# Graph and attention kernel: one block-limit number per group, group release signalled by VectorE, edge weights summed panel by panel

## What is computed

```python
def _rgcn_conv(x, src, dst, etype, W, root, b):
    x_src = x[src]
    seg = dst * num_rel + etype
    sums = jax.ops.segment_sum(x_src, seg, num_segments=num_nodes * num_rel)
    cnt = jax.ops.segment_sum(jnp.ones((src.shape[0],), dtype=x.dtype), seg, num_segments=num_nodes * num_rel)
    mean = sums / jnp.maximum(cnt, 1.0)[:, None]
    mean = mean.reshape(num_nodes, num_rel, -1)
    out = jnp.einsum('nri,rio->no', mean, W)
    return out + x @ root + b
```

## Time and profile before

| | |
|---|---|
| median of 3 runs | 3418.33 us (3415.06 to 3421.1) |
| the profiled execution's own time | 3421.39 us |
| its span, first to last instruction | 3419.5 us |
| edge stage of layer 0 | 650.97 to 1064.3 us of the span |
| edge stage of layer 1 | 1629.93 to 2047.0 us |
| granted TensorE clock, mean | 0.979 |

### The profile page before, as it was taken

How to read it: one execution, slowest core, us unless ns; L and a number is a source line. 1 busy time by engine, 2 the same in 40 slices (tenths; PEclk the granted TensorE clock), 3 DMA queues, 4 the chain that set the end, 5 groups by cost and what they waited for, 6 DMA issues and landing times.

```text
span 3419.5 us, 64810 instructions
## 1 busy us (share of the span) xinstructions
PE 3174.5 (93%) x19556; PEld 2359.9 (69%) x19557; DVE 1773.6 (52%) x2941; ACT 762.8 (22%) x1086; POOL 1273.2 (37%) x1377
## 2 busy tenths in 40 slices
PE   6999999999997999999899989999886999999999
PEld 5788888777776888888677766776654555555555
DVE  7576666555555333333555552334586456455551
ACT  2211121000001212211000004444212543543540
POOL 2681000577772000002777761000420632652562
PEclk9999999999999999999999999999998999999999
DMA  5334334599994232321898882000330000000003
GB/s 149 101 106 149 118 116 137 171 306 307 306 306 140 87 120 94 118 95 63 319 307 307 303 287 78 14 28 14 88 95 24 20 1 19 19 1 19 19 28 95
DMA packets 101141, 433.58 MB, mean 127 GB/s; under 512 B 19648, under 2 KB 19971, under 8 KB 96818
## 3 DMA queue, kind: packets, MB, share of 16 engines
q0 software_dynamic: 55712, 266.87, 23.2%
q1 hardware_dynamic: 42593, 124.83, 11.6%
q10 hardware_dynamic: 2736, 40.50, 3.4%
HBM read 355.21 MB, written 76.88 MB: 126 GB/s over the span
## 4 chain that ended last, share of the span: by engine, by line
PE 71%; DVE 12%; issue 7%; DVEq 6%; ACT 1%; POOL 1%; DMA 1%; POOLq 0%; SPq 0%; ACTq 0%
PE PS L1466 26%; PE PS L1580 13%; PE PS L1776 5%; PE PS L1604 3%; PE PS L1711 3%; PE PS L1475 3%; DVE NM L1387 2%; PE PS L1612 2%; PE PS L1759 2%; PE PS L1760 2%; PE PS L1715 2%; PE PS L1649 2%; DVE HOT L1166 2%; PE PS L1633 2%; PE PS L1623 1%
## 5 line engine op out<-in xcount | busy, mean ns | idle before, releaser
L1466 PE MATMUL PS<-WHL,XT 128*125 (+1 forms) x3240 | 549.4, 329 | 7.0 <-DVE WHL L940 4.2
L1466 PE MATMUL PS<-WHL,HT 128*125 (+1 forms) x3240 | 531.8, 327 | 0.0
L1580 PE MATMUL PS<-GATA,HOT 128*125 128x384 f16 x2880 | 492.6, 328 | 37.0 <-issue 17.8
L1466 PEld LDWEIGHTS PS<-WHL,XT 128*125 (+1 forms) x3240 | 441.3, 138 | 92.7 <-issue 5.3
L1466 PEld LDWEIGHTS PS<-WHL,HT 128*125 (+1 forms) x3240 | 441.9, 137 | 84.2
L558 POOL DMA_INDIRECT GATA<-msg_table,SKEY x432 | 421.8, 976 | 163.0 <-issue 124.6
L1580 PEld LDWEIGHTS PS<-GATA,HOT 128*125 x2880 | 386.3, 137 | 114.5 <-issue 44.6
L1166 DVE SCALAR_TENSOR_TENSOR HOT<-NODE,DSTF,WHLO x720 | 297.0, 475 | 277.6 <-issue 277.6
L594 POOL TENSOR_TENSOR PL<-PF 125x500 bf16<-125x500 f32 (+1 forms) x360 | 320.6, 924 | 281.0 <-ACT PF L797 277.8
L1016 DVE SCALAR_TENSOR_TENSOR MSG<-PS,MSG 125x768 f16<-125x768 f32 x160 | 153.1, 957 | 360.3 <-ACT MSG L627 358.9
L627 ACT ACTIVATE MSG<-PS 125x768 f16<-125x768 f32 x160 | 129.6, 810 | 786.8 <-PE PS L1466 773.9
(11 more groups left out here) (254 smaller groups left out, 3898.6 us busy)
## 6 DMA issues: line engine op xcount, KB each, us to landing
msg_table<-MSG SPq DMA_DIRECT2D x160, 336.0 KB
WST<-in_wg_dram ACTq DMA_DIRECT2D x16, 2304.0 KB, 10.1
WST<-in_wf_dram SPq DMA_DIRECT2D x7, 1536.0 KB, 6.3
KROW<-key_rows POOLq DMA_DIRECT2D x54, 192.0 KB, 3.8
GATA<-msg_table,SKEY POOLq DMA_INDIRECT x432, 4.5
msg_table<-MSG SPq DMA_DIRECT2D x160, 39.0 KB
WST<-in_wm_dram SPq DMA_DIRECT2D x5, 1152.0 KB, 5.1
GATB<-msg_table,SKEY POOLq DMA_INDIRECT x216, 4.5
```

What stands on the lines that cost most here:

```text
L1466: ins = pe.matmul(PS[0:ROWS, b0 + h, 0:HALF], X[:, xp, k, bass.ts(t, ROWS)], panel_part(slot, wp, k, h), start=k == 0 and xp + wp == 0, st ...
L1580: ins = pe.matmul(PS[0:ROWS, bass.ds(((n + (L + 1)) % 2) * 2 + h, 1), 0:HALF].rearrange("p a c -> p (a c)"), HOT[:, bass.ds((n % 2) * AT + ...
```

## The change

- `LIM` holds one number for a group, first block times 10 plus last block; `group_blocks` makes one load and then splits the number in registers with a division and a remainder. This is done by TensorE and by VectorE. `block_limits` computes the packed number once.
- The one-column matmul at the end of a group is gone. VectorE raises `group_used` when it leaves the loop over the group's blocks, and once more after the last take; a group counts as released for GpSimd when the count shows that VectorE has left the loop of the group after it (`grp - GSETS + 2`).
- The drain of VectorE's loop stands now in `take_pass`, behind the `HOT` tiles instead of ahead of them.
- The edge weights are summed by one relation at a time (`relation_weight`): in layer 0 inside the loop that loads the key rows, four relations in panel 3 and then one in each panel, in layer 1 as each panel's scale is ready. When all are there, one multiplication brings them to the common scale (`common_weight`), and three instructions (`edge_weights`) finish. In layer 0 these three come after the first group's four gathers.
- In this diff the order of the nine panels is as before.

```diff
@@ group_blocks
-            return (eng.value_load(LIM[0:1, bass.ds(g, 1)], min_val=0, max_val=RT - 1),
-                    eng.value_load(LIM[0:1, bass.ds(g + AG, 1)], min_val=1, max_val=RT))
+            both = eng.value_load(LIM[0:1, bass.ds(g, 1)], min_val=0, max_val=RT * RT - 1)
+            return both // RT, both % RT + 1
@@ gpsimd
+            def relation_weight(L, r):
+
+                g.wait_ge(S["relation_in"], L * REL + r + 1)
+                g.sem_inc(S["pool_tick"], 1)
+                if r == 0:
+                    g.tensor_scalar(WSUM[:], ETF[:, 0:TILES], 0.0, GW[:, 0:1], ALU.is_equal, ALU.mult)
+                else:
+                    g.tensor_scalar(TMPF[:], ETF[:, 0:TILES], float(r), GW[:, r:r + 1], ALU.is_equal, ALU.mult)
+                    g.drain()
+                    g.tensor_tensor(WSUM[:], WSUM[:], TMPF[:], ALU.add)
+                g.drain()
+
+            def common_weight(L):
 
                 g.wait_ge(S["relations_made"], L + 1)
                 g.sem_inc(S["pool_tick"], 1)
-                g.tensor_scalar(WSUM[:], ETF[:, 0:TILES], 0.0, GW[:, REL:REL + 1], ALU.is_equal, ALU.mult)
-                for r in range(1, REL):
-                    g.tensor_scalar(TMPF[:], ETF[:, 0:TILES], float(r), GW[:, REL + r:REL + r + 1], ALU.is_equal, ALU.mult)
-                    g.drain()
-                    g.tensor_tensor(WSUM[:], WSUM[:], TMPF[:], ALU.add)
-                    g.drain()
+                g.tensor_scalar(WSUM[:], WSUM[:], GS[:, 1:2], None, ALU.mult)
+                g.drain()
+
+            def edge_weights(L):
+
...
+                if u % RT == RT - 1:
+                    p = COUNTED + u // RT
+                    for r in range(0 if p == COUNTED else p, p + 1):
+                        relation_weight(0, r)
+
             for L in range(2):
-                edge_weights(L)
+                if L == 1:
+                    for r in range(REL):
+                        relation_weight(1, r)
+                common_weight(L)
+                if L == 1:
+                    edge_weights(1)
...
+                    if L == 0 and t == AT:
+                        edge_weights(0)
                     if t % AT == 0:
                         if grp >= GSETS:
-                            g.wait_ge(S["group_used"], AG * L + grp - GSETS + 1)
+                            g.wait_ge(S["group_used"], (AG + 1) * L + grp - GSETS + 2)
...
@@ vector
-                v.tensor_scalar(LIM[:, 0:AG], PS[0:1, 5, 0:AG], -1.0, None, ALU.add)
-                v.tensor_copy(LIM[:, AG:2 * AG], PS[0:1, 5, AG:2 * AG])
+                v.tensor_scalar(GBT[:], PS[0:1, 5, 0:2 * AG], -1.0, None, ALU.add)
+                v.drain()
+                v.scalar_tensor_tensor(LIM[:], GBT[:, 0:AG], float(RT), GBT[:, AG:2 * AG], ALU.mult, ALU.add)
...
-                    v.tensor_copy(GW[:, bass.ds(p, 1)], SC[:, WINV])
+                    v.tensor_copy(GW[:, bass.ds(p, 1)], SC[:, WINV]).then_inc(S["relation_in"], 1)
...
-                    v.tensor_scalar(GW[:, REL:2 * REL], GW[:, 0:REL], GS[:, 1:2], W_TOP, ALU.mult, ALU.mult)
+                    v.tensor_scalar(GS[:, 1:2], GS[:, 1:2], W_TOP, None, ALU.mult)
...
                 def take_pass(n):
 
+                    v.drain()
                     v.wait_ge(S["pass_done"], n + (L + 2))
...
                         n = v.snap(cnt, min_val=0, max_val=1 << 20)
-                        v.drain()
                         v.wait_ge(S["pass_done"], n + (L + 1))
...
                         take_pass(n)
                         v.reg_mov(was, b)
                         v.reg_add(cnt, cnt, 1)
+                    v.sem_inc(S["group_used"], 1)
                 v.drain()
                 take_pass(v.snap(cnt, min_val=0, max_val=1 << 20))
+                v.sem_inc(S["group_used"], 1)
@@ tensor
-                        pe.matmul(PS[0:1, 6, 0:1], ZERO[:, 0:1], ZERO[:, 0:1], start=True, stop=True).then_inc(S["group_used"], 1)
```

More of the change, by code:

```diff
@@ L148, in graph_and_attentions_kernel @@
         WHLO = sb(gctx, "WHLO", [128, TILES, 2], f16)
-        GW = sb(gctx, "GW", [128, 2 * REL], f32)
+        GW = sb(gctx, "GW", [128, REL], f32)
         GS = sb(gctx, "GS", [128, 3], f32)
@@ L154, in graph_and_attentions_kernel @@
         CST = sb(gctx, "CST", [128, 171], f32)
+        GBT = sb(gctx, "GBT", [1, 2 * AG], f32)
         GB = sb(gctx, "GB", [AG, 4 + 2 * RT], f32)
-        LIM = sb(gctx, "LIM", [1, 2 * AG], i32)
+        LIM = sb(gctx, "LIM", [1, AG], i32)
         ZERO = sb(gctx, "ZERO", [128, HALF], bf16)
@@ L213, in graph_and_attentions_kernel @@
             edges_in zeros_made bounds_made bounds_t lim_made
-            hot1_made hot1_used cnt_done hir_made hir_out key_in0 key_in1 key_in2 key_in3 key_in4 keys_ready low_made relations_made inverse_made rows2_in keys_made counts_found counts_taken
+            hot1_made hot1_used cnt_done hir_made hir_out key_in0 key_in1 key_in2 key_in3 key_in4 keys_ready low_made relations_made relation_in inverse_made rows2_in keys_made counts_found counts_taken
             hot_made gat_in0 gat_in1 gat_in2 gat_in3 gat_in4 gat_in5 gat_in6 gat_in7 gat_in8 gat_in9 gat_in10 gat_in11 pass_done pass_out group_used weights_made msg_hi rows_done
@@ L406, in _ @@
                 move_rows(sp, gnn_rows[b * ROWS:(b + 1) * ROWS, :], ROOT[:, b, :], S["gnn_out"])
-            sp.wait_ge(S["group_used"], 2 * AG)
+            sp.wait_ge(S["group_used"], 2 * (AG + 1))
             for n_, key in enumerate(("bmp", "gamma", "beta")):
@@ L540, in edge_weights @@
                 g.sem_inc(S["weights_made"], 1)
-            for L in range(2):
-                edge_weights(L)
+            g.wait_ge(S["hir_out"], 16)
+            for u in range(SLOTS):
+                if u >= KRING:
+                    g.wait_ge(S["keys_made"], u - KRING + 1)
+                    g.sem_inc(S["pool_tick"], 1)
+                g.dma_start(KROW[:, u % KRING, :], key_rows[u:u + 1, :].broadcast_to([128, SLOT * 128])).then_inc(S[f"key_in{u % KRING}"], 16)
+                if u % RT == RT - 1:
+                    p = COUNTED + u // RT
+                    for r in range(0 if p == COUNTED else p, p + 1):
+                        relation_weight(0, r)
+            for L in range(2):
+                if L == 1:
[4 more added lines that the diff above has]
+                    edge_weights(1)
                 g.wait_ge(S["msg_out"], ROW_IN * REL * RT * (L + 1))
@@ L547, in _ @@
                     grp, k = t // AT, t % GSLOTS
+                    if L == 0 and t == AT:
+                        edge_weights(0)
                     if t % AT == 0:
                         if grp >= GSETS:
-                            g.wait_ge(S["group_used"], AG * L + grp - GSETS + 1)
+                            g.wait_ge(S["group_used"], (AG + 1) * L + grp - GSETS + 2)
                             g.sem_inc(S["pool_tick"], 1)
                         elif L == 1:
-                            g.wait_ge(S["group_used"], AG)
+                            g.wait_ge(S["group_used"], AG + 1)
                             g.sem_inc(S["pool_tick"], 1)
```

## The result

The changed kernel takes 3441.22 us (median of 4 runs, 3436.79 to 3444.94), the one before 3419.72 us in the same count. The ratio is 1.0062, 95% interval 1.0049 to 1.0075: slower by 21 us, where 19.5 were forecast. Its profiled run has a span of 3435.0 us, at the low end of its runs.

What follows compares the result with a forecast made beforehand. GpSimd's unbroken issue of gathers was taken to bound the edge stages. Late releases, +19.8 us, and starts and ends, -0.3, gave +19.5: 3440.9 us from the profiled 3421.4, 3438 from the median; range 3416 to 3458.

Steps and rivals of the forecast that it cites:

- GpSimd's issue is the bound of the edge stages: Edge stages: GpSimd gathers without a break, 1.283 us each, 5.13 us a group; TensorE catches up and waits.
- The release ahead of a two-pass group is a pass late: Edge stages: VectorE's exit releases the group ahead of each of 18 two-pass groups a whole pass later; +19.8 us, chance 0.52.
- Its size: Stall at each two-pass group: 0.50 + 1.1 - 0.4 = 1.2 us, less today's 0.1; 18 x 1.1 = +19.8 us.
- x: Time from the start of VectorE's take to GpSimd's gather: taken as 1.1 us, 0.9 to 2.0 at the ends.
- 0.50 us of margin: Mean over 18 two-pass groups of the new signal's take start minus today's issue of the gather it gates.
- g: Time by which TensorE starts a two-pass group earlier through the shorter border: taken as 0.4 us, 0 to 0.8.
- The signal doesn't wait for the take: Answers the rival that VectorE's release waits for the take's end, x = 1.9 us: 3454 us, chance 0.16.
- The borders are not the bound: Answers the rival that TensorE and VectorE set the edge stages' pace and shorter borders save 38 us: 3380, chance 0.09.
- The weights in the panels block nobody: Answers the rival that GpSimd's weight instructions block VectorE in layer 0's panels 3 to 7, 17 us: 3455, chance 0.06.
- The limits "otherwise worth nothing": Group borders: packed limits save up to 0.6 us on either engine, but only where gathers are waited for; otherwise 0.
- the starts: Starts of the edge stages: 0 in layer 0, whose first take begins perhaps 0.5 us earlier, +0.5 us in layer 1.
- The drain and the weights: Drain moved to where VectorE waits anyway: 0; edge weights summed by panel: 0 in both layers, 2.4 us upper end.

Runs made afterwards that it cites:

- e7: Kernel before with only the high fp16 half of each message stored, gathered and multiplied (16 matmuls a pass instead of 24): 3416.15 us, ratio 0.9981.
- f1: Kernel before with only the release of a group moved to VectorE's loop exit: 3444.68 us, ratio 1.0063.
- f2: Changed kernel with only the release given back to TensorE's one-column matmul: 3415.5 us, ratio 0.998 to the kernel before.
- e6: Changed kernel with VectorE raising the count at each take, GpSimd waiting for the freed group's last take: 3424.49 us, ratio 1.0016 to the kernel before.
- e5: Changed kernel with a drain ahead of VectorE's release, so that it waits for the take's end: 3476.99 us, ratio 1.0164 to the kernel before.
- f3: Kernel before with only the block limits packed in one number (one load, a division and a remainder): 3415.18 us, ratio 0.9974.
- f4: Kernel before with only the edge weights summed by panel and the first group gathered ahead of the last weight instructions: 3421.29 us, ratio 1.0005.
- e8: Changed kernel with TensorE's release back and edge weights copied to PSUM, so HOT has one SBUF input: 3399.62 us, ratio 0.9931 to the kernel before.

## Why the prediction was right, step by step

- **GpSimd's issue is the bound of the edge stages.** Right, shown by e7.
- **The release ahead of a two-pass group is a pass late.** Right: f1 has the stalls with this part alone, f2 has none of them, and e6, with the pass taken out and VectorE kept as the sender, has 0.30 us at all 18 places.
- **Its size.** x was taken as 1.1 and measured as 1.10 to 1.11 us; the stall as 1.2 and measured, with the 0.30 taken off, as 1.06. With the 0.50 us of margin g comes out as 0.50 + 1.11 - 1.06 = 0.55, not 0.4; it is the remainder, not measured by itself. 18 stalls less those of before are 17.3 us; I had 19.8.
- **The rivals.** The signal doesn't wait for the take: in e5, where it does, x is 1.87 us. The borders are not the bound in layer 0 (f3), but they are near it: 1 us more makes them one (e5). The weights in the panels block nobody (f4).
- **The limits "otherwise worth nothing".** Wrong by 5 us or so: f3 gains 6 to 9. Two terms were missing: the length of the gathers, and the granted clock of the first pass. That pass took 6.83 us before and 5.45 in the changed kernel, whose stretch at 0.50 was half as long; f1 and f4 have nearly the same idle time ahead of it and differ by 1.0 us, so that the change shortened this stretch isn't shown.
- **The gathers' length** is the term that was left out of the sum. I took the rate as fixed at 1.283 us, though a gather is some 0.03 us longer than in e8, where `HOT` has one SBUF input less. With the changed kernel the gathers of layer 0 took 8.2 us more and those of layer 1 2.2 less. So the close hit of the total, 21 against 19.5 us, is in part luck: +17.3 of stalls and +5.9 of gathers, less some us for the starts.
- **The drain and the weights** cost 0, as summed: the weights in f4; the drain's new place was not run by itself, but f2, which has it, is as fast as f3, which doesn't. Of the starts I had only the 0.5 us ahead of the first `HOT`; it was 0.76. I summed layer 0's first released gather to 0, and it began 3.5 us earlier (655.24 instead of 658.71): 1.8 us of it lie ahead of the root panel's end, 0.8 are the border, and 0.9 are what the first pass was faster by, 1.4, less 0.5 for the later signal.

Why did layer 0's gathers get longer and layer 1's shorter in the same kernel? The trace shows where, but not why. Take the gathers that begin within 1.4 us after the first of four `HOT` instructions, and sum what they take above 0.948 us. It is 9.7 and 9.9 us in the two layers before, and 16.4 and 7.3 after, at nearly the same number of such gathers (89 and 91, then 100 and 93). In the last 0.6 us of that time, layer 0 of the changed kernel has 34 gathers of 1.170 us in the mean, layer 1 has 23 of 0.993. So the two engines run in step, and the change moved at which point of the `HOT` instructions a gather falls.

Open: what sets that point. Three kernels with VectorE's release and the moved drain (changed, e5, e6) have 74 or 75 long ones in layer 0, the others with both SBUF inputs 31 to 67; but each was profiled once. And what slowed the first job is not known.

## What to carry to other kernels

When a release signal moves to another engine, ask for each group which event now stands behind it: an average shift of nothing can hide a whole pass in the few groups that have two, and a ring with no slack turns it into a stall of the engine that sets the rate. An engine that never waits still isn't at its floor: look at the spread of its own instructions (0.95 to 1.13 us in the example here) and at what runs beside the long ones. And test the parts of a change one by one: this one held a gain of 7 us and a loss of 28.

## What the runs showed of the hardware

- A gather that begins 0.1 to 1.2 us after the first of four VectorE instructions with two SBUF inputs takes 1.055 us in the mean instead of 0.948 (kernel before, 171 and 461 gathers); with one of the inputs in PSUM (e8) none of 632 takes over 1.0 us.
- An increment that VectorE issues behind a 1.02 us instruction, with no drain between, reaches GpSimd's next gather 1.11 us after that instruction begins (changed kernel), and 1.87 with a drain (e5).
- One register load of a number from SBUF less, and a division and a remainder by 10 more, makes VectorE's border 0.5 us shorter (1.82 to 1.30, f3), so these two together cost 0.5 us less than the load.
- The first pass of 24 matmuls in layer 0, behind 2.4 to 3.2 us of idle time, ran partly at a granted clock of 0.50 and took 5.5 to 6.8 us instead of 4.11. In layer 1, behind 1.8 us of idle time, it took 5.79 us in three kernels (changed, e5, e8) and 4.11, at a granted clock of 1.00, in two (f2, e6).
